# LayerNorm row of an eight-core transformer kernel: 1/sqrt as Ln and Exp on ScalarE in place of Sqrt and a VectorE reciprocal

## What is computed

```
x = x + 0.5 * FFN(LN(x))                  # FFN 1: sigmoid(xr Wr) * (relu(xk Wk)^2 Wv), xr and xk mixed from x and the token before
x = x + Attn(LN(x))                       # below
x = x + 0.5 * FFN(LN(x))                  # FFN 2, same weights

Attn(s):  y  = LN(s, g1, b1)              # a LayerNorm of a LayerNorm
          h  = s + causal attention(y), 16 heads of 64, low-rank weights (48), output by two factors (768)
          return h + gelu(LN(h, g2, b2) fc1U fc1V + b) fc2U fc2V + b

LN(v) = (v - mean(v)) / sqrt(var(v) + eps), over the 1024 features of a token
```

## Time and profile before

| | us |
|---|---|
| median of 2 runs | 2812.72 |
| the two runs | 2798.70 and 2826.74 |
| the profiled execution | 2809.95 |
| its slowest core (core 0), first to last instruction | 2808.4 |
| its other cores | 2781.4 to 2802.3 |

### The profile page before, as it was taken

The page is one execution under the profiler, slowest core; times in us unless marked ns, Lnnn a source line. Parts: engine busy times, 40 slices in busy tenths (PEclk is TensorE's granted clock), DMA queues, the critical chain, the costliest instruction groups (busy, mean ns, idle before and its releaser), DMA issues. The chain is left out here.

```text
span 2808.4 us, 26640 instructions; the slowest of 8 cores (2781.4 to 2808.4 us)
## 1 busy us (share of the span) xinstructions
PE 1679.2 (60%) x5913; PEld 586.0 (21%) x6024; DVE 1039.5 (37%) x1588; ACT 822.2 (29%) x1000; POOL 12.0 (0%) x26
## 2 busy tenths in 40 slices
PE   1446684242676777776776497246666664426885
PEld 0112230000222222222221142012222221002332
DVE  0476734747223323323323113510201001477661
ACT  1112222022254554554554422112222211202221
POOL 0000000000000000000000000000000000000000
PEclk9998895555777877877876797579999998556778
DMA  9000002120200000000003110350000002500002
GB/s 217 3 0 1 1 16 105 45 75 0 46 4 15 14 4 15 14 4 15 3 4 123 27 21 1 53 98 1 1 1 1 1 1 82 128 0 0 1 1 120
DMA packets 7594, 88.10 MB, mean 31 GB/s; under 512 B 1185, under 2 KB 3362, under 8 KB 4642
## 3 DMA queue, kind: packets, MB, share of 16 engines
q0 software_dynamic: 3168, 33.84, 6.9%
q1 hardware_dynamic: 4290, 52.56, 5.2%
HBM read 92.97 MB, written 25.17 MB: 42 GB/s over the span
## 5 line engine op out<-in xcount | busy, mean ns | idle before, releaser
L879 ACT ACTIVATE AT<-sd 128x1024 bf16<-128x1024 f32 x320 | 327.7, 1024 | 232.2 <-PE sd L868 214.6
L916 PE MATMUL pb<-AT,VA 128*65 128x512 bf16 x640 | 228.4, 463 | 122.9 <-DVE QB L823 48.2
L1174 PE MATMUL pq<-HMt,f2U 128*128 128x512 bf16 x503 | 155.0, 382 | 172.4 <-ACT HMt L1167 145.0
L711 PE MATMUL pb<-x,Wu 128*128 128x512 bf16 x735 | 211.2, 435 | 66.1 <-DMA Wu<-Upm 58.9
L1202 DVE SCALAR_TENSOR_TENSOR H<-pq,csts,H 128x512 f32<-128x512 f32 x32 | 24.0, 751 | 480.9 <-PE pq L1194 478.4
L1167 ACT ACTIVATE HMt<-pq,csts 128x512 bf16<-128x512 f32 x128 | 88.0, 687 | 366.5 <-PE pq L1158 366.5
L721 DVE CAST Pq<-pb 128x512 bf16<-128x512 f32 x96 | 66.4, 692 | 282.0 <-PE pb L711 279.8
L868 PE MATMUL sd<-QB,KB 64*128 64x512 bf16 x640 | 130.2, 441 | 63.1 <-ACT AT L879 61.2
L890 DVE TENSOR_TENSOR AT<-AT,bcst 128x512 bf16<-128x512 bf16 x256 | 108.8, 425 | 137.6 <-ACT AT L879 112.5
L1158 PE MATMUL pq<-P1t,f1V 128*128 128x512 bf16 x501 | 133.3, 386 | 7.7 <-ACT P1t L1140 3.8
L916 PEld LDWEIGHTS pb<-AT,VA 128*65 128x65 bf16 x640 | 69.4, 121 | 259.4 <-issue 242.6
(11 more groups left out here) (146 smaller groups left out, 2040.7 us busy)
## 6 DMA issues: line engine op xcount, KB each, us to landing
S<-x_in SPq DMA_DIRECT2D x2, 4096.0 KB, 40.7
H<-spill_h SPq DMA_DIRECT2D x2, 4096.0 KB, 21.6
S<-spill_s SPq DMA_DIRECT2D x2, 4096.0 KB, 19.5
x_out<-S SPq DMA_DIRECT2D x2, 4096.0 KB, 17.1
Wu<-Upm POOLq DMA_DIRECT2D x8, 768.0 KB, 6.3
wkS<-wkT POOLq DMA_DIRECT2D x2, 2048.0 KB, 23.4
wvS<-wvT POOLq DMA_DIRECT2D x2, 2048.0 KB, 38.4
wrS<-wrT POOLq DMA_DIRECT2D x2, 2048.0 KB, 48.6
```

What stands on the lines that cost most here:

```text
L711: p.t(lambda e, tile=tile, m=m, pi=pi, tt=tt, c=c, woff=woff: e.matmul(tile[:, :], Wu[:, woff + 1024 * pi + 128 * c:woff + 1024 * pi + 128 ...
L879: sm = p.s(lambda e, s=s, i0=i0, pp=pp: e.activation(ATb[:, TQ * (4 * s + 2 * pp):TQ * (4 * s + 2 * pp) + 2 * TQ], SD[s][:, :], AF.Exp, sc ...
L916: p.t(lambda e, i=i, h=h, tC=tC, slot=slot, is_last=is_last: e.matmul(tC[0:DH + 1, :], VA[:, VAW * i + 65 * h:VAW * i + 65 * h + 65], ATb[ ...
L1174: p.t(lambda e, tileA=tileA, ic=ic, p2=p2, hslot=hslot: e.matmul(tileA[:, :], f2U[:, 512 * ic + 128 * p2:512 * ic + 128 * (p2 + 1)], HMt[: ...
```

## The change

In the row chain ScalarE's Sqrt and VectorE's reciprocal go. In their place ScalarE computes Ln(bB + eps) in place, and then Exp(-0.5 * bB) in place, which is 1/sqrt(variance + eps). VectorE's product (L380, now L382) waits for ScalarE instead of for its own reciprocal, and the matmuls that spread 1/sigma wait for ScalarE too. A constant, -0.5, is added to the small table of constants that is loaded at the start. `emit_ln` is called five times, so this is done five times. The second LayerNorm ahead of attention uses only the `neg` mark.

```diff
-CONST_VALS = [0.0, 1.0, -1.0, 0.5, 0.125, INVD, EPS]
+CONST_VALS = [0.0, 1.0, -1.0, 0.5, -0.5, 0.125, INVD, EPS]
...
             vv = p.c["V"]
-            sv = p.s(lambda e: e.activation(bB[0:1, :], bB[0:1, :], AF.Sqrt,
-                                            bias=ccol(EPS)[0:1, :], scale=1.0),
-                     wait=[("V", vv)], inc=True)
-            iv = p.v(lambda e: e.reciprocal(bB[0:1, :], bB[0:1, :]), wait=[("S", sv)], inc=True)
+            p.s(lambda e: e.activation(bB[0:1, :], bB[0:1, :], AF.Ln,
+                                       bias=ccol(EPS)[0:1, :], scale=1.0),
+                wait=[("V", vv)], inc=True)
+            sv = p.s(lambda e: e.activation(bB[0:1, :], bB[0:1, :], AF.Exp, scale=-0.5),
+                     inc=True)
+            iv_s = ("S", sv)
             nm = p.v(lambda e: e.scalar_tensor_tensor(
                 statA[0:1, :], statA[0:1, :], -1.0, bB[0:1, :], ALU.mult, ALU.mult),
-                wait=[("V", p.c["V"])], inc=True)
-            return {"inv": iv, "neg": nm}
+                wait=[iv_s], inc=True)
+            return {"inv": sv, "inv_eng": "S", "neg": nm}
...
-            return emit_outer_pair(pool, bB, statA, ("V", r["inv"]), ("V", r["neg"]))
+            return emit_outer_pair(pool, bB, statA, ("S", r["inv"]), ("V", r["neg"]))
```

## The result

| | before | after |
|---|---|---|
| median, us | 2798.76 (10 runs) | 2741.23 (11 runs) |
| lowest, us | 2797.91 | 2738.51 |
| profiled execution, us | 2809.95 | 2741.24 |
| spans of the cores, us | 2781.4 to 2808.4 | 2718.2 to 2739.7 |

After over before is 0.9786, with a 95% interval of 0.976 to 0.9812. Whether it is more than 2% faster stays open, since the interval goes to both sides of 0.98. In microseconds of 2799 the ratio is 60 (53 to 67); the medians alone give 57.5. All ratios in this document compare executions in which neither half of the chip ran at a visibly lower clock.

A forecast was written before the change was run, and what follows sets the result against it. The prediction took a chain of waiting stages as the bound, with the reciprocal running alone. Five savings of 11.02 us, 55.1 in all, from the profiled 2809.95 gave 2755 us, range 2733 to 2784; saving 53 to 57 had chance 0.80.

The forecast's parts named there:

- The bound: Five row chains: nothing else of the program runs beside the 12.94 us reciprocal, 64.7 us in all.
- The sum: One LayerNorm, Sqrt's start to TensorE's start: 15.47 us before, 4.45 after, 11.02 saved; all five 55.1 us.
- The step for the second LayerNorm ahead of attention: TensorE waits there for row products behind L380; Sqrt's end to L380 goes from 13.28 to 2.26 us, 11.02 saved.
- The cover of the product: Product L380: its 2.28 us stay covered by the first tile's spreading matmuls; 2.28 each if cover failed wholly.
- What is late next: Behind each LayerNorm everything moves ahead as one piece; FFN 2's last weights keep 72 us of cover.
- Tables: ScalarE: one table serves Ln and Exp, one load per stage as before at the same place; counted zero.
- Rival A: Row chain: a table switch between Ln and Exp, 1.28 us six times, 7.7 in all, about 2763 us; chance 0.06.
- The level: Whole kernel: sum made against the profiled 2809.95 us; two other runs' median 2.8 higher, those runs 28 us apart.
- the clock at the spreading matmuls: Spreading matmuls: copies' pace is 2.19 us at full and half clock, so shorter idle time gives nothing back; counted zero.
- Rival B: Dense TensorE stretches: the clock gives the saving back, 77.5 us longer, 2832 us, slower than before; chance 0.03.
- Rival C: Row chain: one-partition activations dearer than the Sqrt row, or TensorE late behind ScalarE; saving 49.4, 2760.5 us; chance 0.11.
- D: Weight transfers, longest for FFN 2, take up the saved time; given no room beyond the other rivals.

The follow-up runs named there:

- the three chain lengths: Changed kernel with no reciprocal (0.9786 of before), and with an unread VectorE reciprocal put back between Exp and product: 1x1024 (0.9916) or 1x2048 (1.0022).
- the run with the switch: Against the changed kernel, Sqrt, Ln, then Exp with scale -1 in place of Ln and Exp, forcing a table switch on the row chain: 0.9848 of before.
- the kernel with another 121 us less: Against the changed kernel, four of five LayerNorms make sums with 128 columns of ones, on all partitions, without spreading matmuls: 0.9386 of before, profiled 2620.4 us.

## Why the prediction was right, point by point

**The bound.** That the row chain is bare critical path held: each of the five places gives its time to the end, the three chain lengths lie on a line, and what comes behind a LayerNorm moves ahead as one piece.

**The sum.** 11.02 us a LayerNorm were worked out, 11.11 are in the rows. The 0.09 is Exp, taken as 2.00 from the Sqrt row and really 1.91; it has no bias operand, and in the run with the switch an Ln without one takes 1.91 too; both handovers, 0.09 and 0.36, were as taken, to the hundredth. Sum 55.5 instead of 55.1. The forecast gave its chance to a saving of 53 to 57 us: the rows are inside, the medians' 57.5 and the ratio's 60 (53 to 67) are just above. The step for the second LayerNorm ahead of attention held as well.

**The cover of the product.** Held: it starts 0.18 us ahead of the first matmul as before, and the copies keep 2.19.

**What is late next.** Nothing new. The transfers that TensorE waited for before it waits for after, as long within their scatter (the first use of Wu stands 13.6 us behind its issue before and 14.3 after, medians of the cores). FFN 2's first matmul waits for VectorE's mixing, 37.5 us. By the rows of after its last weights are issued at 2360.9 on core 7, land at 2409 and are used at 2481, 72 us of cover, the number given.

**Tables.** Held: no load on the chain. The reading of attention's loads on the way was not complete. Besides the load at L740 the trace of before has a second one in that stage, on core 0 at 1493.3:

```profile
L879 ACT ACT_TABLE_LOAD x1 | 1.3, 1283 | 3.5 <-PE sd L868 3.5
```

From the first Exp at 760.4 up to that point Ln and Exp take turns without a load, so the conclusion stands; only "one load per stage" was too few, before and after. Rival A, one switch a LayerNorm, was built as a kernel and costs 1.28 a switch, as the rival's price said and not 2.66.

**The level, and the last 2 to 4 us.** This is what was off. The time came out at 2741.2 where 2755 was forecast: 11 us because the profiled execution of before (2809.95) was above the median that ten runs give (2798.8), and 2.4 (by the medians) in stretches whose instructions didn't change. Of the 11 us the rows show nine: on core 0 FFN 2's body took 245.0 us and on core 1 249.2, on the other six cores 235.4 to 235.9. The earlier trace rows had that, and the forecast carried it along in its level; that the wide range still held the time is owed to the room given for the level. I counted zero for the clock at the spreading matmuls, and that is so; but the bursts of statistics matmuls and the first matmuls of a stage do depend on it, by one to three us a stretch in either direction, and so do the waits for transfers. So "the saving is 1.96%" was too exact a statement to put on one side of a 2% line; it came out at 2.14% with an interval of 0.5 points, which leaves the line's side open.

**Rival B** (the saving is given back by the clock). Not seen. The mean granted clock went from 0.773 to 0.789 on before's cores to 0.783 to 0.788, and the kernel with another 121 us less has 0.793 to 0.811. The slow FFN 2 of the earlier trace rows was that execution's own: in after the eight cores take 234.1 to 234.7 us for it.

**Rival C** (activations dearer than the Sqrt row) is out by the rows, and **D** by the covers.

## What to carry to other kernels

Ask of a long instruction whether anything else runs in its window; if every other engine reads zero there, its duration comes off the end one for one, and the sum is as good as its handovers are read. That held here at all five places. An instruction of 2048 fp32 elements costs VectorE 2.28 us on one partition and 2.29 on all 128 (in the changed kernel L371, and L416, which writes bf16), so a chain on one partition behind a reduction is better done broadcast, which here was worth about twice the change itself. And a saving worked out to a tenth of a microsecond is still measured against a level that moves by ten and against stretches that move by one to three without any edit of theirs.

## What the runs showed of the hardware

- The reciprocal of fp32 on VectorE takes 12.94 us for 1x2048 and 6.54 for 1x1024, 6.3 to 6.4 ns an element; a product or difference of the same 2048 takes 2.28.
- A switch of activation tables took 1.28 us on an otherwise waiting chain, with 0.07 and 0.02 us around it, and no further gap.
- A bias read from memory adds 0.09 us to an activation, on one partition (2.00 against 1.908, Ln with and without; Sqrt with it takes 2.00, Exp and Identity without 1.908). On 128 partitions Ln with a bias takes 1.15 and Exp without one 1.06.
- The same 64 matmuls took 29.3 or 32.4 us of busy time on two cores in one execution, by the clock granted, and the stretch around them 54.6 or 56.2.
- A transfer of weights that TensorE waited for took 11.8 to 15.2 us from issue to first use, by core, in two kernels with the same transfers.
